# First-scan scores of a gated two-layer cross-attention kernel: two single PSUM banks in turn, full-height matmuls, and a new order of the work

## The chip, the core and the metric

The kernel runs on one core of a Trainium2 chip. The metric is the device time of one execution in microseconds; the median of several executions is compared.

## What is computed

Sixteen batches of 256 positions with 128 features go through two layers. Each layer is a cross-attention to a context of 1601 rows (16 heads of size 8) and a feed-forward part, both behind tanh gates. Layer 0 attends with a plain softmax, layer 1 keeps the 32 best scores of each row. The feed-forward part of layer 0 is a mixture of 8 experts of width 512, two chosen per position; that of layer 1 is a self-attention plus a mixture of 8 experts of width 128.

```python
# layer 0 attention
scores = einsum('bhqd,bhkd->bhqk', q, k) / sqrt(8)
attn = softmax(scores);  ctx = attn @ v;  out = ctx @ Wo.T + bo
# layer 1 attention
scores = einsum('bhqd,bhkd->bhqk', q, k) / sqrt(8)
top_scores, top_idx = top_k(scores, 32);  w = softmax(top_scores)
out = einsum('bhqk,bhqkd->bhqd', w, top_v) @ Wo.T + bo
# the whole
x = x + tanh(g_xattn[0]) * xattn0(layernorm(x), ctx)
x = x + tanh(g_ffn[0]) * ffn0(layernorm(x))
x = x + tanh(g_xattn[1]) * xattn1(layernorm(x), ctx)
x = x + tanh(g_ffn[1]) * ffn1(layernorm(x))
```

## The kernel before, in words

**Tiling.** The 16 heads of a batch are taken in groups of four (`HG`), so there are 64 groups `g` per layer. Queries come in two tiles of 128 rows (`QT`), keys in 13 chunks of 128 for the weighted sum, or in pieces of up to 512 (`BANK`) for scans. Keys and queries are split into three bf16 parts each, and six products of parts are stacked on the contraction axis: 48 rows (`ROWS`) of head size 8, kept twice in a tile, from partition 0 and from partition 64 (`UP`).

**Stages, by the words of the order.** `w_k`, `w_v`, `w_q`, `u_q` are projections. POOL splits their results (`split`), SP stores them to DRAM (`split_out`) and loads them back (`k_scan`, `k_att`, `q_in`). The *first scan* of layer 0 (`n0`, L589) computes the scores of a row tile against all 1601 keys, and DVE takes the row maximum (`n0_max`, L1024; `n0_all`, L1032). The maximum is turned (`row_turn`), negated (`row_minus`), split (`shift`) and comes back by DRAM as three more rows of q (`rows_out`, `rows_in`), so that the second pass `s_0` (L634) gives scores minus maximum. ACT takes the exponential (`exp_0`, L917), and PE sums with the values (`pv`, L683). Layer 1 scans with `c1` (L604); ACT copies the scores (`c1_out`, L898) into one of five tiles `s`; DVE ranks them in four parts a row tile (`rank`, L946 and the merges L959 to L971), `count` and `check` see whether a part held too many of the best 32 and if so do the ranking again over the whole row (L1071, L1074); `least` makes the threshold. Its second pass is `s_1`, then `cut` on ACT (L907) and `cut_add` on PE (L659) push down what is below the threshold, then `exp_1` and `pv`. `v_w1`, `v_gelu`, `v_w2` and `v_add` are the experts of layer 0; `z_qk`, `z_v`, `z_score`, `z_max` (L772, L1040), `s_z`, `exp_z`, `pv_z` and `z_moe` the last part of layer 1. `ln_*` are layer norms, and `x_add` adds to x.

**What sets the order.** `ORDER` holds, for each of the five engines, one round of words written out: one round is one batch. `LAG` says how many items of a word's stream the first rounds skip, so the stages of different batches overlap and the rounds at both ends are thinner. Each engine runs its list strictly in order. Every step waits on counters of the others. An n0 waits until the maximum of the piece before it is taken, because there is one score tile:

```python
score = psum("score", 2 * BANK)
if i:
    q.wait_ge(sem["score_max"], i)
for x in (1, 0):      # two matmuls, rows 64.. and rows 0.., one bank each
    r = tensor.matmul(score[:, x * BANK:x * BANK + wd], ..., tile_position=(UP * x, 0))
vector.tensor_reduce(m.part[:, ..., c:c + 1], score[:, 0:wd], AX.X, ALU.max)
```

A row tile so takes two pieces: 1024 and 577 columns. `z_score` uses the same tile. The keys of a head for the first scan come in three DMAs (L1393 twice, L1395). The turned, normed rows for layer 0's query projection lie in `oT`, the tile that `o_copy` also uses.

## Time and profile before

| | |
|---|---|
| median of 3 executions | 5482.19 us (5466.11 to 5497.76) |
| the profiled execution | 5491.77 us |
| its span | 5489.7 us |
| busy: PE, DVE, ACT, POOL | 4423.5, 4143.6, 3937.4, 1505.0 us |
| weight loads on PE | 1757.4 us |
| first-scan maxima (L1024) | 1006.1 us in 1024 instructions |
| granted tensor clock | 0.873 of full speed in the mean |
| data moved | 344.97 MB in 472180 packets, 63 GB/s |

Busy time is the union of an engine's instructions, and a busy PE includes the tail of each matmul. Idle time is listed with what ended it; a wait for several counters goes to the one that came last. Idle time of an engine that nothing waits for costs nothing. The chain of waits of this profile reaches back only through the last 85 us, so stretches and waits are read instead.

### The profile page before, as it was taken

How to read it: one execution, taken by the hardware profiler on the slowest of the kernel's cores; microseconds unless marked ns; L12 is line 12 of the kernel's file. 1: busy time of each engine (PE TensorE's matmuls, PEld its weight loads, DVE VectorE, ACT ScalarE, POOL GpSimd, SP SyncE). 2: the span in 40 equal slices, each digit the busy share in tenths (PEclk: the TensorE clock that was granted, in tenths of full speed). 3: DMA queues.
4: the chain of work that ended last, by engine and by line, in shares of the span. 5: the costliest groups of instructions: out<-in, count | busy, mean ns of one | idle time of the engine just before them, and what ended most of it. 6: DMA issues, size and time to landing. Idle time of an engine off the chain costs nothing. (4 is left out here: it accounts for less than half of the span.)

```text
span 5489.7 us, 110897 instructions
## 1 busy us (share of the span) xinstructions
PE 4423.5 (81%) x34296; PEld 1757.4 (32%) x34502; DVE 4143.6 (75%) x21693; ACT 3937.4 (72%) x5166; POOL 1505.0 (27%) x3256
## 2 busy tenths in 40 slices
PE   3677787898788789878878988887898788888665
PEld 1232323242242424224242423324242332424211
DVE  3448687878878787787888788788978878776761
ACT  1346576878677697867869788786979688786673
POOL 3212123232222323222232323132232323131212
PEclk7777788999898899889999989999999899898676
DMA  4222132322223132222323223232323222120100
GB/s 115 73 60 74 41 77 51 76 63 70 61 66 77 48 81 62 67 63 64 77 51 80 62 69 79 56 78 49 86 63 77 60 55 70 47 64 23 37 22 19
DMA packets 472180, 344.97 MB, mean 63 GB/s; under 512 B 155897, under 2 KB 454140, under 8 KB 471550
## 3 DMA queue, kind: packets, MB, share of 16 engines
q1 hardware_dynamic: 471550, 337.54, 24.8%
q8 instruction: 276, 4.52, 0.3%
q14 instruction: 354, 2.90, 0.2%
HBM read 230.12 MB, written 107.13 MB: 61 GB/s over the span
## 5 line engine op out<-in xcount | busy, mean ns | idle before, releaser
L946 DVE MAX8 cand<-s 128x8 f32<-128x67 f32 (+1 forms) x12288 | 1980.0, 221 | 114.2 <-ACT s L898 78.2
L917 ACT ACTIVATE prob<-wide 128x1024 f32<-128x1024 f32 (+1 forms) x1792 | 1753.4, 1030 | 408.9 <-PE wide L634 203.7
L1024 DVE TENSOR_REDUCE part<-score 128x1 f32<-128x1024 f32 (+1 forms) x1024 | 1006.1, 983 | 439.0 <-PE score L589 417.4
L683 PE MATMUL att<-prob,v 128*9 128x256 f32 (+1 forms) x14336 | 1196.9, 413 | 27.7 <-ACT prob L917 27.1
L898 ACT ACTIVATE s<-wide 128x1024 f32<-128x1024 f32 (+1 forms) x1024 | 829.7, 847 | 309.0 <-PE wide L604 210.1
L907 ACT ACTIVATE below<-wide 128x1024 bf16<-128x1024 f32 (+1 forms) x832 | 819.9, 1034 | 107.6 <-PE wide L634 104.2
L634 PE MATMUL wide<-q,k_att 64*128 64x256 bf16 (+1 forms) x6656 | 726.5, 294 | 179.1 <-ACT prob L917 114.1
L1280 POOL TENSOR_SCALAR flag<-cand,ends 128x24 bf16<-128x24 f32 x512 | 177.7, 347 | 2401.9 <-DVE ends L971 1312.9
L589 PE MATMUL score<-k_scan,q 64*128 64x512 bf16 (+1 forms) x2048 | 444.9, 368 | 286.0 <-DVE part L1024 155.4
L604 PE MATMUL wide<-k_scan,q 64*128 64x512 bf16 (+1 forms) x2048 | 427.2, 363 | 205.1 <-ACT prob L917 119.5
L659 PE MATMUL wide<-below,minus_ident 128*128 128x512 bf16 x1458 | 471.2, 399 | 135.3 <-ACT below L907 104.0
L634 PEld LDWEIGHTS wide<-q,k_att 64*128 64x128 bf16 (+1 forms) x6656 | 230.1, 99 | 799.7 <-ACT prob L917 420.7
L683 PEld LDWEIGHTS att<-prob,v 128*9 128x9 f32 (+1 forms) x14336 | 225.7, 90 | 488.2 <-issue 406.6
L738 PE MATMUL small<-w,hid 128*128 128x128 f32 x2048 | 308.6, 296 | 0.0
L589 PEld LDWEIGHTS score<-k_scan,q 64*128 64x128 bf16 x2048 | 103.8, 96 | 593.9 <-issue 359.8
L878 ACT ACTIVATE hid<-wide,b 128x256 f32<-128x256 f32 x512 | 199.2, 477 | 125.4 <-PE wide L725 124.9
L604 PEld LDWEIGHTS wide<-k_scan,q 64*128 64x128 bf16 x2048 | 98.8, 94 | 545.4 <-ACT prob L917 292.4
L738 PEld LDWEIGHTS small<-w,hid 128*128 128x128 f32 x2048 | 258.4, 198 | 32.2 <-issue 2.9
L725 PE MATMUL wide<-v_xnT,w 128*128 128x256 f32 x1024 | 261.5, 403 | 0.0
L971 DVE MAX8 top<-left 128x8 f32<-128x104 f32 x1024 | 256.5, 250 | 0.1
L968 DVE MATCH_REPLACE8 left<-top,left 128x104 f32<-128x104 f32 x1024 | 256.2, 250 | 0.0
L1309 POOL CAST shift<-minus 8x128 bf16<-8x128 f32 x192 | 54.0, 281 | 679.5 <-issue 633.7
(162 smaller groups left out, 5317.4 us busy)
## 6 DMA issues: line engine op xcount, KB each, us to landing
k_stack<-split_b SPq DMA_DIRECT2D x576, 128.0 KB, 2.5
k_att<-k_stack SPq DMA_DIRECT2D x768, 96.0 KB, 2.4
k_scan<-k_stack SPq DMA_DIRECT2D x512, 96.0 KB, 2.3
ctxT<-in_ctx_dram SPq DMA_DIRECT2D x32, 800.5 KB, 4.6
k_scan<-k_stack SPq DMA_DIRECT2D x512, 48.0 KB, 1.8
q<-q_stack SPq DMA_DIRECT2D x256, 96.0 KB
q_stack<-split_b SPq DMA_DIRECT2D x192, 64.0 KB, 2.1
self_stack<-split_b SPq DMA_DIRECT2D x192, 64.0 KB, 2.1
```

The source lines that it names most:

```text
L589: r = tensor.matmul(score[:, x * BANK:x * BANK + wd], m.q[0][g % QBUF[0]][r0:r0 + UP, hh, qt * P:(qt + 1) * P], m.k_scan[0][kn % 2][r0:r0 ...
L604: r = tensor.matmul(ps[:, x * BANK:x * BANK + wd], m.q[1][g % QBUF[1]][r0:r0 + UP, hh, qt * P:(qt + 1) * P], m.k_scan[1][kn % 2][r0:r0 + U ...
L634: r = tensor.matmul(ps[0:kc, j * S:(j + 1) * S], m.k_att[kn % 3][r0:r0 + UP, h, c0:c0 + kc], rows[r0:r0 + UP, j, :], start=(h == 0), stop= ...
L659: r = tensor.matmul(ps[0:kc, x:x + BANK], m.minus_ident[0:kc, 0:kc], m.below[n % 2][0:kc, x:x + BANK], start=False, stop=True, skip_group_ ...
L683: r = tensor.matmul(att[32 * j:32 * j + HD + 1, 0:S], v[0:kc, c, j0 * HG + j, :], m.prob[n % 3][0:kc, j * S:(j + 1) * S], start=(c == 0), ...
L725: r = tensor.matmul(ps[:, k * S:(k + 1) * S], m.w_1[:, e, k * P:(k + 1) * P], m.xnT["v"][:, :], start=True, stop=True)
L738: r = tensor.matmul(ps[:, t * D:(t + 1) * D], hid[:, k, t * P:(t + 1) * P], m.w_2[:, e, k, :], start=False, stop=(k == PT - 1))
L898: scalar.activation(m.s[tile % HELD][:, a0:a0 + wd], ps[:, 0:wd], ACT.Copy).then_inc(sem["wide_done"], 1)
L907: scalar.activation(m.below[n % 2][0:kc, :], ps[0:kc, :], ACT.Relu, scale=-STEEP).then_inc(sem["cut_done"], 1)
L917: scalar.activation(pr[0:kc, :], ps[0:kc, :], ACT.Exp, scale=SCALE).then_inc(sem["wide_done"], 1)
L946: i = vector.max(cand[:, :, c], s[:, KCUT[c]:KCUT[c + 1]])
L1024: vector.tensor_reduce(m.part[:, QT * hh + qt, c:c + 1], score[:, 0:wd], AX.X, ALU.max).then_inc(sem["score_max"], 1)
```

## The change

- `score` becomes two tiles of one bank, used in turn by `n0` and `z_score`. Piece i waits only for the maximum of piece i - 2.
- A row tile of the first scan is four pieces of 512, 512, 512 and 65 columns, each one matmul over all 128 rows. The key tile of layer 0 holds 48 rows once, and the rest is zero. It is loaded by one DMA.
- `z_score` has four pieces of two matmuls for two of four, and `z_max` four maxima.
- The turned rows for layer 0's query projection get the tile `w_xnT`.
- `ORDER` and `LAG` are dealt anew for all engines; one PE round has 573 words for 501, a DVE round 348 for 276. In the changed file the lines are 4 higher at n0 (L593) and 2 higher from z_score (L774) to the maxima (L1026, L1042).

```diff
         m.k_scan = [[sb(f"k_scan{l}_{n}", [P, 2, BANK], BF16) ... for l in range(2)]
+        (layer 0: [P, 1, NK])
-        m.part = sb("part", [P, HG * QT, 2])
+        m.part = sb("part", [P, HG * QT, 4])
-        m.xnT = dict(w=m.oT, v=sb("v_xnT", [P, S]), z=sb("z_xnT", [P, S]))
+        m.xnT = dict(w=sb("w_xnT", [P, S]), v=sb("v_xnT", [P, S]), z=sb("z_xnT", [P, S]))
-        score = psum("score", 2 * BANK)
+        score = [psum(f"score{n}", BANK) for n in range(2)]
...
                     elif name == "n0":
-                        if i:
-                            q.wait_ge(sem["score_max"], i)
-                        for x in (1, 0):
-                            r0, wd = UP * x, min(BANK, NK - (2 * c + x) * BANK)
-                            r = tensor.matmul(score[:, x * BANK:x * BANK + wd],
-                                              m.q[0][g % QBUF[0]][r0:r0 + UP, hh, qt * P:(qt + 1) * P],
-                                              m.k_scan[0][kn % 2][r0:r0 + UP, c, 0:wd], start=True, stop=True,
-                                              tile_position=(r0, 0))
-                        r.then_inc(sem["score_full"], 1)
+                        if i >= 2:
+                            q.wait_ge(sem["score_max"], i - 1)
+                        a0, wd = c * BANK, min(BANK, NK - c * BANK)
+                        tensor.matmul(score[i % 2][:, 0:wd], m.q[0][g % QBUF[0]][:, hh, qt * P:(qt + 1) * P],
+                                      m.k_scan[0][kn % 2][:, 0, a0:a0 + wd],
+                                      start=True, stop=True).then_inc(sem["score_full"], 1)
...
                     elif name == "z_score":
-                        if i:
-                            q.wait_ge(sem["score_max"], i)
+                        if i >= 2:
+                            q.wait_ge(sem["score_max"], i - 1)
+                        x, hx = divmod(h, HALF)
...
                     elif name == "n0_max":
-                        wd = min(2 * BANK, NK - c * 2 * BANK)
-                        vector.tensor_reduce(m.part[:, QT * hh + qt, c:c + 1], score[:, 0:wd], AX.X,
+                        wd = min(BANK, NK - c * BANK)
+                        vector.tensor_reduce(m.part[:, QT * hh + qt, c:c + 1], score[i % 2][:, 0:wd], AX.X,
                                              ALU.max).then_inc(sem["score_max"], 1)
...
                     elif name == "k_scan":
+                        if l == 0:
+                            sync.dma_start(k_scan[0:ROWS, 0, :], stack).then_inc(k_scan_in[l][kn % 2], 16)
+                            continue
```

One line of PE's round, of the words around the experts, before and now:

```
before: ... w_q w_v.0 ln_turn.v s_z n0 s_z route.v v_w1*2 u_turn.1 pv_z*2 c1 n0 v_w2 c1 v_w1 c1 v_w2 c1 v_w1 v_w2 s_0 v_w1 ...
now:    ... route.v n0*2 v_w1*2 flag n0*2 pv.1 row_turn.1 n0 pv.1 c1 n0*3 c1 z_score s_1 v_w2 c1 cut_add n0 v_w2 v_w1*2 ...
```

**PE, the first two row tiles of the first head**, where the pipeline fills. The names are output, keys and queries; a number at the end is the buffer. Before:

```order
L589 MATMUL score<-k_scan0_0,q0_0 128x512 x2
L589 MATMUL score<-k_scan0_0,q0_0 128x65
L589 MATMUL score<-k_scan0_0,q0_0 128x512 x3
L589 MATMUL score<-k_scan0_0,q0_0 128x65
L589 MATMUL score<-k_scan0_0,q0_0 128x512
```

Now:

```order
L593 MATMUL score0<-k_scan0_0,q0_0 128x512
L593 MATMUL score1<-k_scan0_0,q0_0 128x512
L593 MATMUL score0<-k_scan0_0,q0_0 128x512
L593 MATMUL score1<-k_scan0_0,q0_0 128x65
L593 MATMUL score0<-k_scan0_0,q0_0 128x512
```

Before, the pieces are two matmuls (512 with 512, 65 with 512) into one tile; now each is one matmul and the tiles alternate.

**PE, among the experts in a middle round** (L725 is v_w1, L735 and L738 v_w2, L634 s_0, L604 c1, L772 z_score; two lines higher in the changed file from L604 on). Before:

```order
L735 MATMUL small<-b_rows,ones_rows 128x128
L738 MATMUL small<-w,hid 128x128 x4
L634 MATMUL wide<-q_0,k_att 128x256 x4
L725 MATMUL wide<-v_xnT,w 128x256 x4
...
L589 MATMUL score<-k_scan_0,q_1 128x65
L589 MATMUL score<-k_scan_0,q_1 128x512
L725 MATMUL wide<-v_xnT,w 128x256 x4
```

Now:

```order
L727 MATMUL wide<-v_xnT,w 128x256 x8
L782 MATMUL small<-flag,ones_col 1x50
L593 MATMUL score<-k_scan_1,q_1 128x512 x2
L685 MATMUL att<-prob,v_0 9x256 x4
L621 MATMUL small<-ident,th 8x128
L593 MATMUL score<-k_scan_1,q_1 128x65
L685 MATMUL att<-prob,v_0 9x256 x4
L606 MATMUL wide<-k_scan_1,q_1 128x512 x2
L593 MATMUL score<-k_scan_0,q_1 128x512 x3
```

Two v_w1 now stand together, and first-scan pieces, the end of the third pass and c1 fill the space before the first v_w2. Between the first v_w1 and the last v_w2 of a round stand 17 n0 for 3, 12 c1 for 8, 4 z_score for 2, and two w_k, a w_v, a w_q and a cut_add that stood elsewhere.

**DVE, first-scan maxima and rankings in a middle round** (L1024, now L1026, is the maximum; MAX of cand from s and the merges are the ranking). Before:

```order
L964 MAX ends<-cand 128x8
L1024 TENSOR_REDUCE part<-score 128x1
L946 MAX cand<-s 128x8 x3
L968 MATCH_REPLACE left<-ends,cand 128x104
L946 MAX cand<-s 128x8 x3
L971 MAX top<-left 128x8
```

Now:

```order
L1026 TENSOR_REDUCE part<-score 128x1 x13
L948 MAX cand<-s 128x8 x3
L961 MAX cand<-cand 128x8
L948 MAX cand<-s 128x8 x3
L966 MAX ends<-cand 128x8
L948 MAX cand<-s 128x8 x3
L970 MATCH_REPLACE left<-ends,cand 128x104
```

Most maxima stood singly between rankings, with one run of five in a round. Now a round has runs of 11, 12 and 13, each followed by a stretch of rankings.

## Rows read from the trace of the kernel before

**Rows 1.** The page: busy time of each engine; granted tensor clock in 40 slices.

```profile
PE 4423.5 (81%) x34296; PEld 1757.4 (32%) x34502; DVE 4143.6 (75%) x21693; ACT 3937.4 (72%) x5166; POOL 1505.0 (27%) x3256
...
PEclk7777788999898899889999989999999899898676
```

**Rows 2.** Stretches: us, busy PE, PEld, DVE, ACT, POOL, clock, DMA share, GB/s.

```profile
0.00:212.50 212.50, 104.97 (x698) 35.79 (x698) 82.16 (x117) 52.66 (x71) 56.33 (x98) 0.70 0.40 104
212.50:437.80 225.30, 163.82 (x1123) 75.07 (x1122) 111.91 (x394) 97.94 (x140) 43.87 (x77) 0.74 0.26 66
...
2685.70:3004.80 319.10, 260.89 (x2145) 106.40 (x2156) 268.53 (x1365) 245.76 (x324) 93.64 (x202) 0.93 0.27 66
3004.80:3311.90 307.10, 269.61 (x2144) 107.39 (x2156) 246.83 (x1346) 246.13 (x324) 93.65 (x202) 0.92 0.28 69
...
3119.00:3165.00 46.00, 43.94 (x297) 31.21 (x295) 32.43 (x185) 31.78 (x54) 5.61 (x13) 1.00 0.16 40
```

**Rows 3.** Waits (total, times, longest) and a group of the redone ranking, whole span.

```profile
ACT s L898 <- DVEq L1077: 93.2, 6, 21.3
...
L1074 DVE MAX8 top_again<-s 128x8 f32<-128x1601 f32 x32 | 58.5, 1828 | 1.1
```

**Rows 4.** Waits between 3004.8 and 3311.9 us.

```profile
DVE part L1024 <- PE score L589: 17.1, 15, 5.4
...
ACT prob L917 <- PE wide L634: 10.4, 13, 2.6
...
PE wide L604 <- ACT prob L917: 7.6, 14, 1.2
...
PE score L589 <- issue: 5.2, 2, 4.6
...
PE score L589 <- DVE part L1024: 0.2, 1, 0.2
```

**Rows 5.** Timeline of the filling (start, us, [idle before]); waits of L1024, 0 to 437.8.

```profile
57.56 1.23 DVE L1024 TENSOR_REDUCE part<-score 128x1 f32<-128x1024 f32 x1 [23.95 <-PE score L589]
58.84 0.61 PE L589 MATMUL score<-k_scan,q 64*128 64x65 bf16 x2 [1.32 <-DVE part L1024]
59.49 0.76 DVE L1024 TENSOR_REDUCE part<-score 128x1 f32<-128x577 f32 x1 [0.70 <-PE score L589]
60.30 0.61 PE L589 MATMUL score<-k_scan,q 64*128 64x512 bf16 x2 [0.85 <-DVE part L1024]
...
64.43 1.23 DVE L1024 TENSOR_REDUCE part<-score 128x1 f32<-128x1024 f32 x1 [0.79 <-PE score L589]
...
  PE score L589: 184.2, 111
```

**Rows 6.** Groups by form, whole span: count, busy us, mean ns, idle before.

```profile
L1024 DVE TENSOR_REDUCE part<-score 128x1 f32<-128x1024 f32 x512 | 623.0, 1217 | 282.9 <-PE score L589 271.0 <-issue 7.1 <-DVE ends L1074 0.3
L1024 DVE TENSOR_REDUCE part<-score 128x1 f32<-128x577 f32 x512 | 383.1, 748 | 156.1 <-PE score L589 146.5 <-issue 7.9 <-DVE ends L1074 0.3
L1040 DVE TENSOR_REDUCE mx<-score 128x4 f32<-128x1024 f32 x128 | 155.1, 1212 | 29.8 <-PE score L772 27.8
L898 ACT ACTIVATE s<-wide 128x1024 f32<-128x1024 f32 x512 | 528.2, 1032 | 227.1 <-PE wide L604 130.4 <-DVEq L1077 93.2
L907 ACT ACTIVATE below<-wide 128x1024 bf16<-128x1024 f32 x768 | 754.7, 1035 | 103.3 <-PE wide L634 102.1
```

**Rows 7.** Timeline of PE in the steady part.

```profile
3008.40 0.38 PE L659 MATMUL wide<-below,minus_ident 128*128 128x512 bf16 x1 [0.16 <-issue]
3008.96 0.61 PE L659 MATMUL wide<-below,minus_ident 128*128 128x512 bf16 x2 [0.18 <-ACT below L907]
...
3141.82 0.39 PE L589 MATMUL score<-k_scan,q 64*128 64x65 bf16 x2
```

**Rows 8.** Timeline of SP and PE around PE's wait for layer 0's queries.

```profile
3183.62 0.78 SPq L1375 DMA_DIRECT2D q<-q_stack  x2
...
3186.54 0.61 PE L589 MATMUL score<-k_scan,q 64*128 64x512 bf16 x2 [4.62 <-issue]
```

195 lines of the change are left out of this document (98 added, 97 removed), and 10 rows, old and new, of tables (act, sp).

## The prediction

> **What bounds the kernel now.** I read the profile in this order: the page for the shares, the table by stretches for the rhythm, the groups by form for prices, the waits of one steady stretch, and the timeline where the score tile is handed over. The page [rows 1] shows no engine full: PE 81%, DVE 75%, ACT 72%. The tensor clock is the second thing to see there: 7 in the first five slices, 8 or 9 from there to the last three. The stretches [rows 2] are cut at every 64th maximum of the first scan, that is one batch each. The first two are the pipeline filling (212 and 225 us, DVE busy 82 and 112), fourteen middle ones take 300 to 335 (two of them shown), and the rest is the pipeline emptying. In a middle stretch of 307.1 us PE is busy 269.6, DVE 246.8, ACT 246.1. The one before it took 319.1, with the same ACT time and 21.7 us more of DVE.
>
> That difference is the ranking done again (L1071, L1074): three replacements and three maxima over 1601 columns at 1.8 us for each of two tiles, 22 us. One wait of up to 21.3 us then stands on ACT [rows 3]. So a DVE delay of 20 us reaches the end, but smaller ones do not: in the 307 us stretch DVE waits 17.1 us for PE's scores, while PE waits 0.2 us for DVE's maximum [rows 4]. PE's own waits there are on ACT (7.6 us at L604 the largest sum) and one of 4.6 us before a first-scan score. ACT in its turn waits on PE (10.4 us at L917) [rows 4]. The steady state is therefore an exchange between ACT (the s_1, cut and exp words) and PE (the feed-forward words, where it is busy 43.9 of 46 us, row for 3119 to 3165 [rows 2]). DVE has 60 us a batch to spare.
>
> The filling is different. There nothing covers the scan, and PE and DVE alternate on the one score tile [rows 5]: 0.61 us of matmul, 1.23 us of maximum, 0.61, 0.76, with DVE idle 0.70 and 0.79 between. Two row tiles take 64.43 - 57.56 = 6.87 us, 3.43 each. Of the first 128 maxima (two batches, 64 row tiles) 111 waited for PE, 184.2 us in all [rows 5].
>
> **The change, part by part.**
> *Filling, the handover.* A handover costs 0.70 to 0.79 us [rows 5], so 111 of them are 83 us; the other 101 us of the 184 are keys or queries not yet there, which the change does not touch. With two banks the matmul of the next piece runs under the maximum of this one, so the 83 go. Two things come back. First, DVE's work: 1217 ns for 1024 columns and 748 for 577 [rows 6] make 1.05 ns a column and 143 ns fixed, so a piece of 512 costs 680 ns and one of 65 costs 211. A row tile is 3 x 680 + 211 = 2251 ns against 1965, 0.286 more; 64 x 0.286 = 18 us. Second, behind the short piece the next matmul (0.61 + some 0.09 of handing over at this clock) is not hidden by 0.21 us: 0.5 us a row tile, for 56 of 64 (111 of 128) 28 us. Sum -83 + 18 + 28 = **-37 us**. Ends: if the denser PE lifts the clock, the matmul takes the 0.39 us seen in the steady rows [rows 7], the exposed part halves and it is -51; if in the second stretch the work of batch 0 sets the pace, only the first stretch's half is saved and the rest is lost to the longer maxima, -10. I take -37: the rows of both filling stretches show the same 0.70.
>
> *Steady state, PE.* A pair of 64-row matmuls takes the same time whether it is 512 + 512 or 512 + 65 columns (both 0.61 in the filling [rows 5], 0.39 later [rows 7]), so the two run together. Two full-height ones behind one another take 0.61 against 0.38 for one [rows 7], so each further 512 columns cost 0.22. A row tile was two passes, 0.44, and is 3 x 0.22 + 0.04 = 0.70: 0.26 more, 512 times, 133 us or 8.3 a batch. The Trainium skill, "TensorE: Matmul & The Clock Gate", section "Back-to-back issue gap", gives some 131 ns for a 512-column matmul in a stream of loads and matmuls; by it a row tile would grow by 0.17 and not 0.26 us, 87 in place of 133 us. The trace's 0.61 - 0.38 disagrees, and I go by the row. The second score (L772) gives up its pairs too: 128 pieces become 256, some 0.2 us more for each old one, 27 us or 1.7 a batch. Together 10 us a batch on PE. Where ACT is the pace it is hidden: two chunks of the third pass are two cuts at 1.03 and two exponentials of as many columns, 4.1 us of ACT [rows 6], for six short groups of matmuls of 0.4 to 0.6 us. If ACT were faster it would not be. In the feed-forward words PE is the pace. Between the first v_w1 and the last v_w2 of a batch the new order has 17 n0 for 3, 12 c1 for 8, and two w_k, a w_v, a w_q and a cut_add that stood elsewhere: PE 14 x 0.22 + 4 x 0.22 and about 3 for the rest, +7 us. But the ACT work that came along (four c1_out at 1.03 or, for 577 columns, some 0.65; a cut at 1.03; four drains of half as many columns or fewer, some 0.5 each) is an estimated 3.4 + 1.0 + 2.2 = 6.6 us [rows 6] that leaves the part where ACT is the pace. I take **0**. Ends: all 10 us a batch on the path, +140 over fourteen stretches; or the move of ACT work worth more than the passes, -5 a batch, -70.
>
> *Steady state, DVE.* 512 x 0.286 = 147 us on L1024, and L1040 goes from 128 x 1212 ns to 256 x 680, +19: 166 us, 10.4 a batch [rows 6]. It stands beside 60 us of idle time and loses most of the 17 us of waiting [rows 4], **0**. If that cover were gone, it would be +10 a batch. What is queued behind a late maximum is the ranking, then check, which gives ACT its s tiles back.
>
> *SP.* k_scan for layer 0 is one DMA in place of three: 512 issues of about 0.4 us fewer (two took 0.78 [rows 8]), some 13 us of SP a batch. PE's 4.62 us wait ends at 3186.54, when a q load has landed that SP issued at 3183.62 [rows 8]. In the new order q_in.0 has the same k_att in front of it and 7 PE words in place of 9 to cover it. **0**; ends -5 and +5 a batch.
>
> *The buffer of its own for layer 0's turned rows* takes away a tie between ln_copy and o_copy, which no row shows as a wait: **0**. The redone rankings keep their 20 us.
>
> Sum: 5491.8 - 37 = 5454.8 us for the profiled execution. It was 9.6 us above the median of the runs shown, so **5445 us**, 0.7% less.
>
> **The rivals.**
> *Slower: DVE's rankings are bunched.* The new DVE order has runs of 11 to 13 maxima and then eight to fourteen ranks with no maximum among them. A rank is some 1.2 us (DVE's 246.8 us [rows 2] less 63 for the first scan's maxima and some 30 for the rest, over 128), so fourteen are 17 us in which PE can pass two score pieces and no third. Before, maxima lay singly between ranks, and there was one run of five. For it: a 22 us DVE delay goes straight to the end [rows 3], DVE rises to 257 of 307. Against it: PE's words over the same stretch hold about 20 us of ACT work. It decides from the point where a bunch is longer than that ACT work; if each of the four bunches of a batch sticks out by 2 us, and PE's passes in the feed-forward words add to it, the price is the 8.3 us a batch of the passes: 14 x 8.3 = 116, 5445 + 116 = **5561 us**.
> *Faster by more: the new order closes steady waits too.* PE's 4.6 us wait and some of ACT's 10 us ones [rows 4] shrink by 5 us a batch, and the filling gains 51: 5482 - 51 - 70 = **5361 us**. For it: two pieces of run-ahead let PE issue scores where it has time. Against it: PE waits only 0.2 us for maxima now.
> *Hardly anything:* the filling is paced by key stores and loads, which the 101 us of other waiting allow; -10, **5472 us**.
>
> **How the numbers follow.** Chances: forecast 0.40, bunched ranks 0.30, steady waits closed 0.17, hardly anything 0.13. Less than 0.5% is about what a measurement of this kernel cannot tell from no change; its edge is at 5455. The forecast's own spread (5430 to 5470) gives 0.32 of its 0.40 to faster, the rest to same. Faster 0.32 + 0.17 = 0.49, same 0.08 + 0.13 = 0.21, slower 0.30. The range takes in both outer cases with their centres and part of their spread: 5350 to 5580.
>
> **What would show it.** Right: the maximum of 512 columns near 680 ns (1536 of them), of 65 near 211; DVE's wait for scores in the first two batches from 184 to about 130 us and the 128 old maxima's time range, 57 to 438, shorter by about 37; PE busy up by 100 to 160 us with middle stretches still 300 to 335. Wrong: middle stretches of 315 and more without a redone ranking, PE waiting several us a batch for a maximum, or DVE above 270 in them (then the bunches are the cause); middle stretches under 300 (then the order has closed waits); or one n0 matmul not costing 0.22 behind another.

## The result and the profile after

The change made the kernel slower: 5572.7 us (5566.1 to 5582.2, 4 runs) against 5474.2 us (5448.6 to 5497.8, 4 runs) in the same session, a ratio of 1.0182 with a 95% interval of 1.0131 to 1.0233. The forecast was 5445. The profiled execution took 5577.55 us, its span 5575.6. All medians below leave out three executions of two later kernels (5763, 6999 and 7425 us) that fell in a slower state of the chip.

The page of the changed kernel: busy time, tensor clock, DMA, then three groups.

```profile
PE 4636.0 (83%) x34502; PEld 1863.9 (33%) x34502; DVE 4231.1 (76%) x22845; ACT 3933.6 (71%) x5164; POOL 1511.5 (27%) x3256
...
PEclk7778889999897999889899998989998898988676
...
DMA packets 427129, 344.97 MB, mean 62 GB/s; under 512 B 135417, under 2 KB 396796, under 8 KB 426494
...
L1026 DVE TENSOR_REDUCE part<-score 128x1 f32<-128x512 f32 (+1 forms) x2048 | 1103.9, 566 | 500.1 <-PE score L593 472.7
...
L900 ACT ACTIVATE s<-wide 128x1024 f32<-128x1024 f32 (+1 forms) x1024 | 821.4, 843 | 353.7 <-PE wide L606 203.9
...
L593 PE MATMUL score<-k_scan,q 128*128 128x512 bf16 (+1 forms) x2048 | 682.3, 366 | 257.0 <-DVE part L1026 177.3
```

Against [rows 1] PE is busy 212.5 us more, DVE 87.5 more, ACT 3.8 less. For PE 100 to 160 us had been said; the trace of before lacks 206 of its 34502 matmul records, so its 4423.5 is somewhat low. The clock's digits are alike and its mean is 0.872 after 0.873, so these two profiles alone say nothing of the clock; set beside the same pieces in the old order it will matter. By form, the price of the maxima came out as forecast, 684 and 213 ns:

```profile
L1026 DVE TENSOR_REDUCE part<-score 128x1 f32<-128x512 f32 x1536 | 1018.2, 684 | 461.7 <-PE score L593 435.5 <-issue 13.8 <-DVE ends L1076 1.3
...
L1026 DVE TENSOR_REDUCE part<-score 128x1 f32<-128x65 f32 x512 | 109.3, 213 | 38.4 <-PE score L593 37.2
```

Where the time went shows in three long stretches, cut at the first maximum, at the first maximum of batches 3 and 15, and at the end (columns as in [rows 2]). Before the change:

```profile
57.60:756.60 699.00, 497.45 (x3585) 199.76 (x3596) 430.29 (x1791) 356.84 (x476) 141.26 (x273) 0.75 0.26 66
756.60:4565.90 3809.30, 3212.31 (x25718) 1290.55 (x25872) 3114.52 (x16267) 2951.39 (x3877) 1123.57 (x2424) 0.91 0.27 67
4565.90:5489.70 923.80, 699.73 (x4951) 259.01 (x4988) 582.68 (x3604) 622.58 (x803) 215.81 (x512) 0.80 0.15 37
```

After it:

```profile
59.70:753.90 694.20, 527.19 (x3575) 207.33 (x3574) 447.76 (x2023) 348.43 (x471) 143.33 (x277) 0.79 0.26 67
753.90:4626.20 3872.30, 3364.31 (x25873) 1377.60 (x25872) 3178.87 (x17130) 2951.76 (x3876) 1128.49 (x2424) 0.91 0.25 66
4626.20:5575.60 949.40, 730.91 (x5012) 270.74 (x5010) 586.57 (x3658) 626.69 (x805) 215.32 (x508) 0.79 0.14 36
```

The first three batches are 4.8 us shorter, where 37 were expected. The twelve middle ones are 63.0 us longer, 5.2 each, where nothing was expected. The end is 25.6 longer. (The profiled execution of the kernel before was some 15 us above the median of its executions in the later sessions, so its stretches are long by about that much in sum.) Yet the handover itself did what was forecast. The timeline of DVE at the start of the changed kernel:

```profile
59.74 2.22 DVE L1026 TENSOR_REDUCE part<-score 128x1 f32<-128x512 f32 x4 [26.81 <-PE score L593]
...
62.54 2.22 DVE L1026 TENSOR_REDUCE part<-score 128x1 f32<-128x512 f32 x4 [0.57 <-PE score L593]
...
65.39 2.22 DVE L1026 TENSOR_REDUCE part<-score 128x1 f32<-128x512 f32 x4 [0.64 <-PE score L593]
```

A row tile takes 2.80 and 2.85 us in place of 3.43 [rows 5]; the forecast's terms make 3.43 - 1.30 + 0.286 + 0.44 = 2.86. So some 0.6 us for each of 64 row tiles was gained and lost again elsewhere in the same stretch.

Two things in the middle are new. First, the experts: from a batch's first v_w1 to its last v_w2. Two such stretches of the changed kernel (columns as above):

```profile
2822.80:2881.10 58.30, 56.53 (x357) 38.64 (x357) 45.84 (x265) 39.15 (x66) 13.10 (x24) 1.00 0.18 45
3136.60:3194.80 58.20, 56.43 (x356) 38.55 (x357) 45.81 (x265) 39.07 (x66) 13.10 (x24) 1.00 0.18 45
```

and two of the kernel before:

```profile
2816.00:2866.00 50.00, 47.94 (x320) 34.71 (x320) 35.29 (x202) 32.46 (x55) 7.56 (x15) 1.00 0.17 43
3116.90:3166.90 50.00, 47.94 (x320) 34.72 (x320) 35.28 (x202) 32.45 (x55) 7.56 (x15) 1.00 0.17 43
```

PE is busy 97% of the time in them in the changed kernel and 96% before, at full clock, and 8.5 us of added work are 8.2 to 8.3 us of added time. Second, the wait behind the redone ranking [rows 3], in the groups of the changed kernel by line:

```profile
L900 ACT ACTIVATE s<-wide 128x1024 f32<-128x1024 f32 (+1 forms) x1024 | 821.4, 843 | 353.7 <-PE wide L606 203.9 <-DVEq L1079 143.3 <-PE wide L636 0.5
...
L1076 DVE MAX8 top_again<-s 128x8 f32<-128x1601 f32 x32 | 58.5, 1829 | 1.1
```

The ranking is redone as often (32 maxima), but ACT now waits 143.3 us for it, 14 times, in place of 93.2 and 6 times. ACT's idle time before L900 grows by 44.7 us in all (309.0 before).

### The profile page after: what moved, and what is told of

Its sections match the earlier page's. It is cut to its first block and busy times, and to the rows that moved or that the text cites. A ratio compares the mean times of both kernels' runs of the same rounds, so it can differ in the third digit from the quotient of the medians.

```text
span 5575.6 us, 111825 instructions
## 1 busy us (share of the span) xinstructions
PE 4636.0 (83%) x34502; PEld 1863.9 (33%) x34502; DVE 4231.1 (76%) x22845; ACT 3933.6 (71%) x5164; POOL 1511.5 (27%) x3256
## 5 line engine op out<-in xcount | busy, mean ns | idle before, releaser
L1026 DVE TENSOR_REDUCE part<-score 128x1 f32<-128x512 f32 (+1 forms) x2048 | 1103.9, 566 | 500.1 <-PE score L593 472.7
L685 PE MATMUL att<-prob,v 128*9 128x256 f32 (+1 forms) x14336 | 1182.2, 407 | 15.1 <-ACT prob L919 12.8
L900 ACT ACTIVATE s<-wide 128x1024 f32<-128x1024 f32 (+1 forms) x1024 | 821.4, 843 | 353.7 <-PE wide L606 203.9
L593 PE MATMUL score<-k_scan,q 128*128 128x512 bf16 (+1 forms) x2048 | 682.3, 366 | 257.0 <-DVE part L1026 177.3
L636 PE MATMUL wide<-q,k_att 64*128 64x256 bf16 (+1 forms) x6656 | 711.7, 291 | 210.1 <-ACT prob L919 139.3
L606 PE MATMUL wide<-k_scan,q 64*128 64x512 bf16 (+1 forms) x2048 | 443.4, 379 | 193.2 <-ACT s L900 124.4
L661 PE MATMUL wide<-below,minus_ident 128*128 128x512 bf16 (+1 forms) x1664 | 511.1, 394 | 32.3 <-ACT below L909 30.3
L636 PEld LDWEIGHTS wide<-q,k_att 64*128 64x128 bf16 (+1 forms) x6656 | 214.1, 97 | 785.5 <-ACT prob L919 490.8
L593 PEld LDWEIGHTS score<-k_scan,q 128*128 128x128 bf16 x2048 | 186.6, 98 | 699.6 <-DVE part L1026 368.5
L1295 POOL CAST split_b<-split_f 128x512 bf16<-128x512 f32 (+2 forms) x192 | 92.7, 483 | 688.4 <-issue 646.5
L727 PE MATMUL wide<-v_xnT,w 128*128 128x256 f32 x1024 | 245.2, 388 | 0.0
```

The lines of the kernel that those rows point to most:

```text
L593: tensor.matmul(score[i % 2][:, 0:wd], m.q[0][g % QBUF[0]][:, hh, qt * P:(qt + 1) * P], m.k_scan[0][kn % 2][:, 0, a0:a0 + wd], start=True, ...
L606: r = tensor.matmul(ps[:, x * BANK:x * BANK + wd], m.q[1][g % QBUF[1]][r0:r0 + UP, hh, qt * P:(qt + 1) * P], m.k_scan[1][kn % 2][r0:r0 + U ...
L636: r = tensor.matmul(ps[0:kc, j * S:(j + 1) * S], m.k_att[kn % 3][r0:r0 + UP, h, c0:c0 + kc], rows[r0:r0 + UP, j, :], start=(h == 0), stop= ...
L661: r = tensor.matmul(ps[0:kc, x:x + BANK], m.minus_ident[0:kc, 0:kc], m.below[n % 2][0:kc, x:x + BANK], start=False, stop=True, skip_group_ ...
L685: r = tensor.matmul(att[32 * j:32 * j + HD + 1, 0:S], v[0:kc, c, j0 * HG + j, :], m.prob[n % 3][0:kc, j * S:(j + 1) * S], start=(c == 0), ...
L900: scalar.activation(m.s[tile % HELD][:, a0:a0 + wd], ps[:, 0:wd], ACT.Copy).then_inc(sem["wide_done"], 1)
```

## The experiments

Six theories recur in the expectations. ORDER: the new order costs the time. PASSES: PE's two more passes a row tile cost it. MAXIMA: DVE's added work costs it. QUERIES: the load of layer 0's queries is late. LOADS: issues of key transfers on SP cost time. FEED-FORWARD: PE work among the experts costs its full price. Every ratio is to the kernel before in the same session. Its median there was 5476.9, 5478.9, 5484.0, 5471.5 and 5478.1 us in the five sessions (the runs of one session: the two orders and two forms of pieces; three loads, joined maxima and the two third tiles; the kernel before with the third tile, less work and the second score; filling only, joined and more work; the last two). So a difference between runs of different sessions is known to some 10 us, and where the ratios give another value than the medians, both are told. The changed kernel itself was measured only in the session of the result, four times; its ratio is known to 0.5%, some 28 us.

Every execution also has its mean granted clock, and time and clock go together: in the 24 executions of the kernel before in one session, the fastest took 5443.0 us at 0.883 and the slowest 5513.0 at 0.869, and a line through all of them falls by 3.8 us for each 0.001 of clock. Below, the clock is given where two kernels differ in it by more than their executions do among themselves.

### Mechanism and order apart

**Old order, new pieces.** Everything of the change except the orders:

```diff
-ORDER: new          LAG: n0 255, n0_max 256, z_score 80, z_max 80
+ORDER: the one before, each n0, n0_max, z_score, z_max written twice
+LAG:   the one before, these four doubled (254, 256, 80, 80)
```

> Everything of the change (two single banks in turn, four full-height pieces, one key transfer, own buffer) but the orders: the old ORDER with every n0, n0_max, z_score and z_max word written twice, and their lags doubled. Theory ORDER (the time was lost because the new order puts words where PE and ACT wait more, queries above all): this kernel is at the old time or under it, 5430 to 5480 us. Theory PASSES (two more full-height passes a row tile, 8.3 us a batch of PE, lie on the path): 5550 to 5600 us as with the change, PE busy some 4630. Theory MAXIMA (the 10.4 us a batch of added DVE work lies on the path): also 5550 to 5600, with DVE's waits for PE's scores gone.

Measured: **5494.8 us**, ratio 1.0032 (1.0012 to 1.0051), 15 us above the range of ORDER and 55 below that of PASSES and MAXIMA. The order costs 78 of the 96 us (82 by the ratios), the pieces 18. Its long stretches:

```profile
57.10:725.20 668.10, 500.30 (x3543) 206.01 (x3596) 442.13 (x1983) 357.94 (x476) 141.44 (x273) 0.81 0.26 70
725.20:4565.70 3840.50, 3259.16 (x25501) 1333.03 (x25872) 3173.90 (x17131) 2961.53 (x3877) 1125.38 (x2424) 0.92 0.26 66
4565.70:5491.00 925.30, 710.00 (x4933) 268.10 (x4988) 588.61 (x3700) 623.26 (x803) 216.26 (x512) 0.80 0.14 37
```

Here the filling is 30.9 us shorter than before the change. DVE's waits for scores between 57 and 446 us were 184.2 [rows 5]. They are 120.5 in this kernel and 163.7 in the changed one, the first row and the second:

```profile
DVE part L1024 <- PE score L591: 120.5, 67, 22.6
```

```profile
DVE part L1026 <- PE score L593: 163.7, 80, 26.8
```

So the new pieces give some 31 us in the filling and the new order takes 26 of them back in the first three batches, in longer waits: one of 18.45 us at 170.8 us is the longest after the first. The middle stretches are 31 us longer than before by the pieces, and 32 more by the order; the end is 24 longer by the order alone. The 31 us of the filling are not the handover alone. The denser PE also lifted the clock there, as the prediction's first end had it: the trace has the lower level, 1.2 GHz, for 252 us of that stretch, for 343 before. The next version but one, with 64-row pieces and three key transfers, has it for 310 us and its filling is only 18 us shorter (680.8 us).

The clock also separates the two orders. With the same pieces and the same work the executions had 0.881 to 0.888 under the old order and 0.870 to 0.875 under the new. In the middle stretch PE stood at the lower level for 611 us under the old order and 713 under the new, and was busy 105 us more under the new (372 matmul records are missing from the first of the two). At 3.8 us for 0.001, an estimate from the executions of the kernel before, the 0.012 would be 46 of the 78 us. Whether the clock fell because the new order makes PE wait in other places, or whether it is most of the cost itself, no run here separates.

**New order, old pieces.** The kernel before with the new order, in which of each two n0, n0_max, z_score and z_max words the second is kept.

> The other half: the kernel before, with the one two-bank tile and the 64-row pairs, under the new order, in which of each two n0, n0_max, z_score and z_max words the second is kept. Theory ORDER: it keeps the loss, 5540 to 5600 us. Theory PASSES or MAXIMA: it loses the added work and keeps the order, 5440 to 5490 us.

Measured: 5718.6 us, ratio 1.0468 (1.0427 to 1.0509), above all the ranges. This one tells little. In the new order o_copy stands between ln_copy and w_q, and with one `oT` for both, layer 0's queries come from other rows. That changes the data: the ranking is redone 18 times in place of 16. The one two-bank tile also ties PE to an order made for two; its mean clock is 0.850. What it does show is why the change gives the turned rows a tile of their own: the new order can't do without it.

**Old order, 64-row pieces in single banks.** The two pieces of a pair stand behind one another.

```diff
-                        tensor.matmul(score[i % 2][:, 0:wd], m.q[0][g % QBUF[0]][:, hh, qt * P:(qt + 1) * P],
-                                      m.k_scan[0][kn % 2][:, 0, a0:a0 + wd],
-                                      start=True, stop=True).then_inc(sem["score_full"], 1)
+                        tensor.matmul(score[i % 2][:, 0:wd], m.q[0][g % QBUF[0]][r0:r0 + UP, hh, qt * P:(qt + 1) * P],
+                                      m.k_scan[0][kn % 2][r0:r0 + UP, c // 2, 0:wd],
+                                      start=True, stop=True, tile_position=(r0, 0)).then_inc(sem["score_full"], 1)
```

> As the old order doubled with the two single banks in turn, but each piece is a 64-row matmul, in turn on rows 0 and rows 64 (keys in the old layout with three transfers), so that the two of a pair stand behind one another and can run together. PE's extra passes are gone, DVE's four maxima stay. Theory PASSES: 5430 to 5480 us, some 100 under the same with full-height pieces. Theory MAXIMA: no better than that one, 5550 to 5600. Theory ORDER: 5430 to 5480 for both.

Measured: 5513.3 us, ratio 1.0072 (1.0046 to 1.0098), that is 18 above the full-height version. No theory had said that; the version with three key transfers, below, explains it. Its clock is lower too, 0.868 to 0.874.

**New order, 64-row pieces.** The same edit to the changed kernel.

> The changed kernel with its new order, but with 64-row pieces and the old key layout with three transfers. Only 275 of 1024 pairs stand behind one another in the new order, so at most 275 x 0.22 = 60 us of PE work go. Theory PASSES: 5510 to 5550 us. Theory ORDER or MAXIMA: 5560 to 5580, as the changed kernel; if the single key transfer had been worth something, above that.

Measured: 5580.6 us, ratio 1.0194 (1.0165 to 1.0224), beside 5573 for the changed kernel, as ORDER and MAXIMA had it. Beside the last one it is a second measure of the order, both in one session: 67 us, at 0.860 against 0.870.

### Loads, maxima and queries

**Three key transfers.** Old order and full-height pieces; the one transfer is cut by columns at 512 and 1024.

```diff
-                            sync.dma_start(k_scan[0:ROWS, 0, :], stack).then_inc(k_scan_in[l][kn % 2], 16)
+                            for c0, c1 in ((0, 512), (512, 1024), (1024, NK)):
+                                sync.dma_start(k_scan[0:ROWS, 0, c0:c1], stack[:, c0:c1]).then_inc(k_scan_in[l][kn % 2], 16)
```

> The old order doubled, full-height pieces, but each head's keys of the first scan come by three transfers in place of one, cut by columns. The one with 64-row pieces and three transfers was 18 us slower than the one with full-height pieces and one, though its PE had less to do. Theory LOADS (three issues on SP cost those 18 us and hide a gain of the shorter PE work): 5510 to 5530 us. Otherwise 5490 to 5500 us, and the 18 us belong to the pieces of 64 rows themselves.

Measured: 5519.4 us, ratio 1.0075 (1.0051 to 1.0098), as LOADS had it. The single transfer of the change is worth 25 us by the medians and 24 by the ratios, for which the prediction had taken 0. Against this one the 64-row version (5513.3) is 6 us faster by the medians and 2 by the ratios: at equal loads PE's shorter work gives next to nothing here, though at a clock of 0.870 against 0.884.

**Joined maxima.** Old order, full-height; from group 8 on two pieces are issued together and one maximum goes over both banks.

```diff
+                        if g >= SINGLE and n % 2 == 0:
+                            continue
...
+                        for x in (1, 0) if g >= SINGLE else (0,):
+                            ...
+                        r.then_inc(sem["score_full"], 2 if g >= SINGLE else 1)
...
+                                vector.tensor_reduce(m.part[:, QT * hh + qt, c:c + 1], both[:, 0:wd], AX.X,
+                                                     ALU.max).then_inc(sem["score_max"], 2)
```

> Old order doubled, full-height pieces, one key transfer; from the third batch on (group 8) the two pieces of a pair are issued together and one DVE maximum goes over both banks, as before the change (1024 and 577 columns). So in the steady part PE keeps the extra passes and DVE loses the extra 10 us a batch; the filling keeps the two banks in turn. Measured for the old order doubled: 5495 us, filling (first three stretches) 669 us, twelve middle stretches 3842 us against 3810 before. Theory PASSES: middle stretches stay at 3840, 5495 us or a little more. Theory MAXIMA: they return to 3810, 5460 us.

Measured: 5496.7 us, ratio 1.0035 (1.0013 to 1.0058), the same as with single maxima (5494.8, ratio 1.0032). Theory MAXIMA falls: 129 us of DVE work less change nothing that can be told.

**A third query tile.** One line and one number, first in the changed kernel:

```diff
-QBUF = (2, 3)
+QBUF = (3, 3)
-    "q_in.0": 7,
+    "q_in.0": 6,
```

> The changed kernel with a third query tile for layer 0, and each q_in.0 one group earlier on SP. In the changed kernel the chain back through the middle spends some 125 us more on query transfers and SP than under the old order, since the query load waits for the last s_0 of two groups back and only 7 words of PE cover it. Theory QUERIES (this wait is what the new order costs): 5490 to 5530 us. Theory FEED-FORWARD (the n0 words among the experts, where PE is the pace, are what it costs): 5550 to 5575 us, the waits on q gone and others in their place.

Measured: 5522.9 us, ratio 1.0089 (1.0057 to 1.0120), 50 less than the changed kernel. There PE had waited 47.4 us for query transfers before first-scan matmuls, 24 times; with the third tile it never does. Then under the old order with the new pieces:

> The old order doubled (5495 us) with the same third query tile and earlier q_in.0. There the chain spends only 20 us on query transfers and SP. Theory QUERIES and theory FEED-FORWARD: 5475 to 5495 us, that is little; a gain of more than 30 us would say that queries are late in either order.

Measured: **5423.7 us**, ratio 0.9893 (0.9859 to 0.9926). Both theories were wrong here: it gains 71 us, more than under the new order. So queries are late in either order, and this can't be what the new order costs. With the third tile the two orders stand 99 us apart, a third measure of the order, in one session. Their middle stretches and their waits behind the redone ranking, old order first:

```profile
707.90:4487.70 3779.80, 3223.66 (x25502) 1329.26 (x25872) 3171.82 (x17131) 2954.07 (x3877) 1123.80 (x2424) 0.93 0.26 67
...
L898 ACT ACTIVATE s<-wide 128x1024 f32<-128x1024 f32 (+1 forms) x1024 | 834.9, 844 | 320.9 <-PE wide L604 218.5 <-DVEq L1077 93.3 <-PE wide L634 0.9
```

```profile
734.40:4582.60 3848.20, 3299.98 (x25585) 1372.59 (x25871) 3175.06 (x17130) 2949.77 (x3877) 1124.90 (x2425) 0.91 0.26 66
...
L900 ACT ACTIVATE s<-wide 128x1024 f32<-128x1024 f32 (+1 forms) x1024 | 820.7, 842 | 353.9 <-PE wide L606 197.8 <-DVEq L1079 150.2 <-PE wide L636 0.5
```

The middle is 68 us longer, and 57 us more of waiting stand behind the redone ranking, of which ACT gets 21 back in shorter waits for PE at the same line. But the clock differs as well, 0.891 to 0.897 against 0.869 to 0.876, and in the middle PE stood at the lower level for 505 us under the old order and for 713 under the new.

**The kernel before with the third query tile**, the same two edits.

> The kernel before, with nothing but a third query tile for layer 0 and each q_in.0 one group earlier. Theory QUERIES (a query load of layer 0 was late in the old order too, and the two banks in turn have no part in it): 5410 to 5445 us against 5479. Rival HANDOVER (the third query tile gained 71 us under the doubled old order because the pieces there run ahead and want the queries sooner): 5465 to 5480 us.

Measured: **5394.1 us**, ratio 0.9827 (0.9803 to 0.9851). Theory QUERIES holds, and the single banks have no part in it: it is even below the range. What first-scan matmuls and their weight loads (PEld, a track of its own beside PE's) waited for, over the whole span (total, times, longest), in the kernel before:

```profile
PEld score L589 <- issue: 359.8, 426, 23.5
...
PE score L589 <- DVE part L1024: 155.4, 116, 23.1
PE score L589 <- issue: 64.3, 35, 4.7
```

and with the third tile:

```profile
PEld score L589 <- issue: 269.7, 418, 23.5
...
PE score L589 <- DVE part L1024: 156.2, 112, 23.1
```

The wait of 4.62 us in [rows 8] reads "issue" too, though the query load had just landed: of the two counters that a head's first piece waits for, none is named. PE itself had 35 such waits, 64.3 us, and with the third tile not one; the weight loads' idle time of that name, which can lie beside busy matmuls, falls by 90 us. Whether the gain comes from the queries alone is open: with two tiles SP, which issues in order, also has to stand still at q_in.0 until the last s_0 of two groups back, with every other load behind it.

### PE's work among the experts and elsewhere

**Taking work away.** In the changed kernel, 195 first-scan matmuls of 512 columns do 65.

```diff
+                        if key in short:
+                            wd = 65
                         tensor.matmul(score[i % 2][:, 0:wd], m.q[0][g % QBUF[0]][:, hh, qt * P:(qt + 1) * P],
```

> The changed kernel (5573 us) with its new order; those 195 first-scan matmuls of 512 columns that stand between a batch's first v_w1 and its last v_w2 do 65 columns only, so the row maxima miss these scores (the work of 447 columns is left out each time); DVE's maxima stay as they are. From the first v_w1 to the last v_w2 a batch took 58.3 us in the changed kernel and 50.7 under the old order. Theory FEED-FORWARD (PE is the pace there, and each n0 word put there costs its full price): the 58.3 become some 56, and the time falls by 195 x 0.18 = 35 us to 5538. Rival (PE's passes are hidden there as elsewhere): 5570 us.

Measured: 5612.0 us, ratio 1.0243 (1.0214 to 1.0271), 39 us *more* with less work by the medians and 33 by the ratios. The stretches among the experts, two neighbours:

```profile
2179.00:2242.60 63.60, 60.79 (x358) 43.08 (x357) 45.68 (x264) 39.13 (x66) 12.97 (x24) 0.89 0.16 42
2516.80:2574.20 57.40, 54.53 (x357) 38.48 (x357) 45.17 (x261) 39.08 (x66) 12.98 (x24) 1.00 0.19 46
```

Where the clock stayed at its upper level, 2.4 GHz, PE was busy 2.0 us less and the 58.3 us became 57.4, 0.9 less. In six of the twelve stretches of the middle batches 0.89 or 0.94 was granted in the mean, and they took some 60 or 63.6. The fall lies inside the stretch, the slices of the one before these:

```profile
1862.00:1870.00 8.00, 7.17 (x53) 4.39 (x53) 6.75 (x28) 6.68 (x15) 0.53 (x2) 1.00 0.07 20
1870.00:1878.00 8.00, 8.00 (x32) 5.83 (x32) 5.96 (x39) 2.67 (x4) 1.49 (x5) 0.56 0.28 73
1878.00:1886.00 8.00, 8.00 (x30) 6.79 (x29) 3.00 (x19) 3.91 (x6) 0.00 (x0) 0.59 0.00 0
1886.00:1896.00 10.00, 9.00 (x57) 5.59 (x55) 7.75 (x42) 6.08 (x14) 0.61 (x2) 1.00 0.05 12
```

PE was busy 7.17 of the 8 us ahead of the fall, and then all the time at 0.56 and 0.59, near the lower level, 1.2 GHz. In the stretch that began at 2516.8 the same words met the same 7.17 of 8 us and the clock stayed:

```profile
2516.80:2524.80 8.00, 7.17 (x53) 4.39 (x53) 6.76 (x28) 6.68 (x15) 0.54 (x2) 1.00 0.08 21
2524.80:2532.80 8.00, 7.95 (x52) 6.33 (x52) 6.60 (x45) 5.04 (x6) 1.48 (x5) 1.00 0.31 73
```

So this experiment mixed two effects and could not tell what it was made for. **Less work elsewhere:**

> The same with 195 other first-scan matmuls of 512 columns, those that come next after each batch's last v_w2, among the third pass, the cuts and the exponentials, done with 65 columns (again the row maxima miss these scores). Theory FEED-FORWARD: ACT is the pace there, so 5565 to 5575 us, next to nothing. Rival (PE is the pace everywhere): 35 us less here too, 5538.

Measured: 5571.3 us, ratio 1.0152 (1.0125 to 1.0179), as FEED-FORWARD had it. Taking 35 us of PE work from among the exponentials gave 2 us by the medians and 16 by the ratios. In the same session it is 41 us under the one with the short pieces among the experts.

**Adding work.** To the old order with the third tile (5423.7 us), 225 passes more.

```diff
-                        tensor.matmul(score[i % 2][:, 0:wd], ...).then_inc(sem["score_full"], 1)
+                        for _ in range(4 if key in again else 1):
+                            r = tensor.matmul(score[i % 2][:, 0:wd], ...)
+                        r.then_inc(sem["score_full"], 1)
```

> The old order doubled with the third query tile (5424 us); each of the 75 first-scan matmuls of 512 columns that stand among the experts (five a batch, between its first v_w1 and last v_w2) is issued four times in place of once, the same result written again: 225 more passes of 0.22 us, 50 us of PE, 3.3 us a batch. Theory FEED-FORWARD (PE is the pace there, so words put there cost their full price): 5465 to 5475 us, 50.8 us a batch there become 54. Rival (hidden): 5420 to 5430 us.

Measured: **5477.1 us**, ratio 1.0008 (0.9988 to 1.0029): by the medians 53 us, by the ratios 63, for 50 us of work. A stretch among the experts with it, then one where the added work stands elsewhere:

```profile
3074.80:3127.60 52.80, 52.07 (x335) 36.73 (x334) 36.74 (x208) 32.36 (x55) 6.52 (x15) 1.00 0.15 37
```

```profile
3064.60:3115.40 50.80, 48.80 (x319) 35.22 (x319) 36.62 (x208) 32.40 (x55) 6.54 (x15) 1.00 0.15 38
```

PE is busy 3.3 us more, the stretch only 2.0 longer; the rest of the 3.5 us a batch comes behind it. The clock is full in both stretches, but not over the whole: this kernel had 0.883 to 0.888, the one without the added work 0.891 to 0.897, and in the middle PE stood at the lower level for 625 us in place of 505. So adding work moved the clock as well, and how much of the 53 us is work and how much clock stays open. **More work elsewhere:**

> The same 225 more passes, 50 us of PE, on 75 other first-scan matmuls of 512 columns: the five that come next after each batch's last v_w2, among the exponentials and cuts. Theory FEED-FORWARD (ACT is the pace there): 5424 to 5435 us. Rival (PE's work costs its full price everywhere, as theory PASSES has it): 5465 to 5475 us.

Measured: **5460.3 us**, ratio 0.9969 (0.9951 to 0.9986): 37 us by the medians, 42 by the ratios, for the 50; measured side by side it is 17 us under the one with the work among the experts. It lies between the two theories, nearer to the rival. Its mean clock, 0.891 to 0.897, is that of the kernel without added work. So right behind the experts PE's work costs three quarters of its price or more, and "ACT is the pace there, so PE's words are free" is wrong. Among the experts the whole cost, clock included, is the full price.

### The rest of the pieces, and the best version

**Second score joined again**, on the old order with the third tile: z_score and z_max over both banks as before the change.

> The old order doubled with the third query tile (5424 us), where z_score and z_max go back to pairs over both banks with one maximum of 1024 columns, as before the change. PE and DVE have 1.7 and 1.2 us a batch less to do there. Theory SECOND SCORE (the four single pieces of the second score cost more than they save): 5395 to 5410 us. Otherwise 5418 to 5428 us.

Measured: 5403.6 us, ratio 0.9854 (0.9828 to 0.9880). The single pieces cost 20 us, of 27 us of PE work that the prediction had counted and put at 0.

**The same with joined maxima as well**, and **single banks in the first two batches alone** with 64-row pairs behind them:

> The old order doubled with third query tile and joined second score (5404 us), and with joined maxima from group 8 on: PE's full-height passes and the one key transfer stay, DVE is back to its old work. Theory MAXIMA (the 147 us more of DVE cost something in the steady part): 5385 to 5395 us. Theory PASSES: 5400 to 5408 us, and the kernel with 64-row pairs is 20 us or more under it.

Measured: 5406.1 us, ratio 0.9875 (0.9837 to 0.9914), as PASSES had it, and not below the one with single maxima (5403.6).

> The kernel before with the third query tile (5394 us), and single banks in turn in the first two batches alone (64-row pieces, three key transfers); from group 8 on, and for the second score throughout, everything as before the change. Theory FILLING (the hand-over in the first two batches is worth what it was forecast to be, here 19 us between the first three stretches of the two kernels with the third tile, 655 and 674 us): 5370 to 5380 us. Rival (the filling is paced by keys once queries are early): 5390 to 5400 us.

Measured: 5374.9 us, ratio 0.9811 (0.9777 to 0.9845). It is 19 us under the kernel before with the third tile by the medians and 9 by the ratios, as theory FILLING said or half of it (the filling itself is 16 us shorter, 657.6 against 674.0), and in the same session 31 under the one with full-height passes (35 by the ratios), though it makes three key transfers to its one.

**Two key transfers**, and then **single banks throughout**, still with 64-row pieces:

```diff
+                            sync.dma_start(k_scan[UP:UP + ROWS, 0, BANK:NK], stack[:, BANK:NK]).then_inc(k_scan_in[l][kn % 2], 16)
+                            sync.dma_start(k_scan[0:ROWS, 0, 0:3 * BANK], stack[:, 0:3 * BANK]).then_inc(k_scan_in[l][kn % 2], 16)
```

> As the version with single banks in turn in the first two batches alone (5375 us), but a head's first-scan keys come by two transfers in place of three (columns 0 to 1535 to the lower rows, 512 to 1600 to the upper), more bytes in fewer issues. Theory LOADS (three issues in place of one cost 26 us under the old order without the third query tile): 5358 to 5368 us. Rival (with queries early, SP is late nowhere): 5370 to 5380 us.

Measured: 5366.6 us, ratio 0.9807 (0.9783 to 0.9830); 8 us under the one with three by the medians, 2 by the ratios, less than can be told.

```diff
-SINGLE = 8
+SINGLE = 64
```

> The same with single banks in turn and four maxima a row tile in all batches, still with 64-row pieces side by side, so that PE has no pass more. DVE has 8 us a batch more than in the version with two loads. Theory MAXIMA (DVE's longer work sits on the path): 40 us or more above that version. Rival (hidden): within 10 us of it.

Measured: **5363.1 us**, ratio 0.9796 (0.9772 to 0.9819). Measured side by side with the joined maxima, the four maxima cost nothing: MAXIMA fails again. This is the fastest version here, 2.0% under the kernel before and 3.8% under the changed one: old order doubled, a third query tile, two single banks in turn with 64-row pieces side by side, two key transfers, the second score joined. Against the full-height version (5403.6) the middle shows where PE's passes went, this one first:

```profile
713.60:4438.10 3724.50, 3196.17 (x25874) 1285.40 (x25872) 3158.67 (x17035) 2945.09 (x3877) 1128.07 (x2424) 0.93 0.29 73
```

```profile
711.00:4480.70 3769.70, 3262.39 (x25874) 1313.13 (x25872) 3161.53 (x17035) 2954.55 (x3877) 1123.91 (x2424) 0.93 0.27 68
```

The DVE work is the same, PE is busy 66 us less, and the middle is 45 us shorter, at a slightly lower clock (0.885 to 0.888 against 0.893 to 0.897).

## Why the prediction was wrong

**Filling, handover: right in kind, -37 forecast.** Under the old order the three first stretches are 30.9 us shorter and DVE's waits for scores are 120.5 where about 130 was said. Part of the 30.9 is the clock, and 4 is the single key transfer (671.7 us with three); with 64-row pieces it was 18, and kept to the filling alone the single banks gave 9 to 19 us with the queries early. And the term was taken without asking what the new order does to the filling: it gives 26 of them back. In the changed kernel DVE's waits are 163.7, so that sign failed.

**Steady PE, the step that failed.** The prediction put 10 us a batch of PE work at 0: "Where ACT is the pace it is hidden". Added work showed the price: 37 us for 50 of work where ACT was thought the pace, at an unchanged clock, and 53 for 50 among the experts, with a loss of clock in it. PE's passes themselves cost 41 us by the medians (5403.6 - 5363.1) and 32 by the ratios, though the full-height version had one transfer less, of 133 forecast as work. With two query tiles they cost only 6 us or 2 (5519.4 - 5513.3). The second score cost 20 of 27.

**The balance in the feed-forward words, the larger miss.** The +7 us of PE there was near: 58.3 us against 50.0 to 50.8 where the clock was full. The 6.6 us of ACT work that leaves the rest was to pay for it and did not. From one batch's last v_w2 to the next one's first v_w1 the changed kernel shows some 264 us in the mean of eleven, the one with the old order 268: 4 less, and no less where both have the third tile (262 in both). In these parts PE stands at the lower level for 59 us a batch under the new order, for 50 under the old, and for 59 and 41 with the third tile. So the clock, which the prediction left out of the steady part, is one candidate for what ate the 6.6 us, and the longer wait behind the redone ranking another; the cause stays open between them. With the third query tile the two orders differ by 99 us, of which 68 lie in the middle, 25 in the first three batches.

**Rankings.** "The redone rankings keep their 20 us" was wrong: their work stays, but ACT's wait for them went from 93.2 to 143.3 us, and 6 waits became 14. That the new order covers them less, and that this comes from the bunched ranks, is argued from the order and not tested. The steady wait of PE for maxima, the sign named for the rival with bunched ranks, is not there: 177.3 us over the whole span where it was 155.4 before, and in the stretch from 3030.6 to 3342.6 us of the changed kernel 1.7 us, with DVE busy 252 of 312. Taking DVE's added work out under the old order changed nothing. The rival's number, 5561, was near, which is luck as far as PE's waits for maxima go: its price was the passes in the feed-forward words, taken in as an addition.

**Steady DVE at 0: right** under the old order, shown with two query tiles and with three (5496.7 against 5494.8; 5363.1 against 5366.6); under the new order it was not tried.

**SP and queries at 0: wrong in both.** One key transfer for three gave 25 us where 0 with 5 a batch to either side was said. And the one wait of 4.62 us in [rows 8] was read and dismissed, though the trace has 35 waits of that name on PE before first-scan matmuls, 64.3 us in all; a third tile was worth 1.7% of the kernel before, 90 us in its session.

**One matmul's price.** 15 more passes in a batch made PE busy 3.3 us longer, 0.22 us each, as the forecast took from [rows 7]. The Trainium skill, "TensorE: Matmul & The Clock Gate", section "Back-to-back issue gap", gives some 131 ns in a stream of loads and matmuls; these passes disagree with it and stand near the 216 ns that the same section gives for an isolated one.

Summed up, by medians: pieces under the old order +18 (filling about -31, of which 4 by the single key transfer, the rest of that transfer -21, second score +20, passes and what remains +50), the new order +78; the forecast had -37 and 0. The +50 is the remainder of the others, not measured by itself, and the passes measured alone are 2 to 41 of it.

## What to carry to other kernels

Before work on an engine is called hidden because another one is the pace, repeat it: issue some of its instructions again at that place and time it. Compare the mean granted clock of the two kernels as well: taking work away moved it here (0.872 to 0.859), and so did adding it among the experts (0.894 to 0.885), while adding it elsewhere did not. Only the last of these gives a price of the work alone. A short wait that comes back at the same place in every round and reads "issue" is worth one cheap try with a buffer more, before any larger rebuild. And where a change brings a mechanism and a new order together, run the mechanism under the old order first: here it separated 18 us from 78, and showed that the order changed the clock with the work left as it was.

## What was not expected of the hardware

Less PE work gave a lower clock: with 195 matmuls cut short, the mean granted clock fell from 0.872 to 0.859, and stretches that ran at 1.00 twelve times of twelve in the changed kernel were at 0.89 or 0.94 in six of twelve, PE busy 7.17 of the 8 us ahead of the fall that was looked at. Such a stretch took some 60 or 63.6 us in place of 57.4. The 64-row pieces, also less PE work, ran at 0.870 beside 0.884 for full-height ones with as many loads. But it is no rule: more work among the experts lowered the clock too. Why one stretch fell and its like did not stays open.

A new order of the same work moved the clock as much: 0.884 to 0.872, 0.870 to 0.860 and 0.894 to 0.873 in the three pairs measured, beside 78, 67 and 99 us.

The number of key transfers mattered: three with the same bytes as one cost 24 to 25 us. Bytes mattered less, if at all: two transfers with 1.6 times those bytes cost no more than three (5366.6 against 5374.9).
